# Building the upper list from a complement that GpSimd writes, in the second attention of a two-layer model

## The reference, cut to what matters

```python
draft = jnp.einsum('bhqd,bhkd->bhqk', qr, kr)
causal_future = qi[:, None] < ki[None, :]
draft = draft + jnp.where(causal_future, neg, jnp.asarray(0.0, dtype))
num_remain = max(min(Sq, MIN_REMAIN), Sq - int(Sq * MASK_OUT))     # 128
_, draft_indices = jax.lax.top_k(draft, num_remain)
mask = mask.at[b_idx, h_idx, s_idx, draft_indices].set(0.0)
mask = jnp.where(causal_future[None, None, :, :], neg, mask)
scores = jnp.einsum('bhqd,bhkd->bhqk', qr, kr) / np.sqrt(HD).astype(np.float32) + mask
attn = jax.nn.softmax(scores, axis=-1)
out = jnp.einsum('bhqk,bhkd->bhqd', attn, v)
```

## Time and profile before

| | us |
|---|---|
| median of 3 runs (2258.46 to 2261.43) | 2259.57 |
| the profiled execution | 2258.43 |
| its span | 2256.6 |
| TensorE matmuls busy | 1860.4 (82%) |
| VectorE busy | 1500.8 (67%) |
| ScalarE busy | 1181.4 (52%) |
| GpSimd busy | 802.9 (36%) |

### The profile page before, as it was taken

How to read it: one execution, slowest core, us unless ns; L and a number is a source line. 1 busy time by engine, 2 the same in 40 slices (tenths; PEclk the granted TensorE clock), 3 DMA queues, 4 the chain that set the end, 5 groups by cost and what they waited for, 6 DMA issues and landing times. The chain is left out here.

```text
span 2256.6 us, 27824 instructions
## 1 busy us (share of the span) xinstructions
PE 1860.4 (82%) x8600; PEld 1331.2 (59%) x8600; DVE 1500.8 (67%) x3325; ACT 1181.4 (52%) x2969; POOL 802.9 (36%) x523
## 2 busy tenths in 40 slices
PE   5898999988999769999765777778777777777997
PEld 4777777777777648887652443333444333335885
DVE  3677777777777644555652788888788888723335
ACT  3556656566565432333326677876677676242221
POOL 3445445455453435565321111112311112123442
PEclk9999999999999979999775778879887888887998
DMA  4011111111110112221240000010000000001111
GB/s 159 25 53 60 65 67 43 52 59 71 60 47 21 61 56 102 94 84 56 98 105 17 15 15 15 15 29 11 18 15 15 15 15 15 0 0 52 51 42 51
DMA packets 48722, 104.11 MB, mean 46 GB/s; under 512 B 6672, under 2 KB 30864, under 8 KB 44432
## 3 DMA queue, kind: packets, MB, share of 16 engines
q1 hardware_dynamic: 48624, 102.95, 13.7%
HBM read 95.59 MB, written 7.34 MB: 46 GB/s over the span
## 5 line engine op out<-in xcount | busy, mean ns | idle before, releaser
L225 PE MATMUL PS<-XT,AR 128*128 128x512 f32 x2472 | 620.2, 406 | 25.9 <-POOL AR L833 12.3
L225 PE MATMUL PS<-AR 128*128 128x512 f32 (+2 forms) x2568 | 540.7, 365 | 24.8 <-POOL AR L342 13.2
L225 PEld LDWEIGHTS PS<-XT,AR 128*128 128x128 f32 x2472 | 471.3, 193 | 139.4 <-issue 16.7
L225 PEld LDWEIGHTS PS<-AR 128*128 128x128 f32 x2568 | 441.5, 192 | 117.8 <-POOL AR L342 16.2
L1436 POOL TENSOR_TENSOR AF<-AF 128x512 f32<-128x512 f32 (+3 forms) x64 | 148.4, 2320 | 675.0 <-DVE AF L1668 675.0
L1610 DVE MAX8 BF<-PS 128x8 f32<-128x256 f32 (+2 forms) x384 | 196.7, 555 | 60.7 <-PE PS L1233 59.1
L1376 ACT ACTIVATE AF<-PS 128x512 f32<-128x512 f32 x160 | 92.5, 595 | 268.6 <-PE PS L1244 191.5
L1258 PE MATMUL PS<-AF,BF 128*128 128x512 f32 x320 | 190.3, 699 | 28.8 <-ACT AF L1376 28.6
L586 POOL TENSOR_TENSOR AF<-AF 128x512 f32<-128x512 f32 (+1 forms) x64 | 107.5, 1680 | 169.2 <-DVE AF L717 169.2
L580 POOL TENSOR_TENSOR AF<-AF 128x512 f32<-128x512 f32 x80 | 103.3, 1292 | 169.3 <-ACT AF L372 169.3
L1212 PE MATMUL PS<-AR,XT 48*128 48x128 f32 (+3 forms) x256 | 94.9, 454 | 73.3 <-DVE BF L1538 40.7
(11 more groups left out here) (195 smaller groups left out, 3451.2 us busy)
## 6 DMA issues: line engine op xcount, KB each, us to landing
AF<-in_mean_w SPq DMA_DIRECT2D x48, 448.0 KB, 3.3
AF<-in_ffn_w SPq DMA_DIRECT2D x14, 1536.0 KB, 6.6
AF<-in_attn_w SPq DMA_DIRECT2D x9, 1536.0 KB, 8.1
XT<-rope_scratch SPq DMA_DIRECT2D x180, 64.0 KB, 2.8
AF<-in_attn_w SPq DMA_DIRECT2D x9, 1024.0 KB, 5.0
AF<-in_ffn_w SPq DMA_DIRECT2D x11, 769.0 KB, 4.2
rope_scratch<-BF SPq DMA_DIRECT2D x20, 256.0 KB, 2.3
AF<-in_x SPq DMA_DIRECT2D x8, 256.0 KB, 4.1
```

Of the source, the lines that this page charges most:

```text
L225: last = nc.tensor.matmul(dst, lhs(a, c), rhs(m, c), start=(first and k == 0), stop=(k == 3 * n - 1 and not more))
```

## The change

GpSimd gets a third task, `complement`: it reads each mark as soon as it is written and writes mark minus one, 0 where marked and -1 elsewhere, in bf16 into one of two buffers `rest`. 2^126 times this is the same as what L1226 and L1228 build with two matmuls, so one matmul of `big_b` with `rest` takes their place. Its sixteen instructions for a tile stand in GpSimd's code ahead of the tile's four `norm`; from the third head on each also waits until TensorE has read the buffer two heads before. On TensorE the two matmuls of the under list now come first, then the wait for `rest`, then the one matmul of the over list, then the two score matmuls. The constant `less_big` and ScalarE's conversion of it go.

```diff
-        less_big = SG[:, 1536:2048]
+        rest = [SG[:, 1536:2048], SG[:, 3328:3840]]
...
-            pe.wait_ge(A1["mask_b"], 5)
+            pe.wait_ge(A1["mask_b"], 4)
...
+                pe.wait_ge(A1["above"], 16 * before(x) + h + 1)
+                under = slot(listed(x, h, 0))
+                nc.tensor.matmul(under[:, 0:W], negbig_b, above[:, h % 3, 0:W], start=True, stop=False)
+                nc.tensor.matmul(under[:, W - P:W], ident_b, mask_b, start=False, stop=False)
+                pe.wait_ge(A1["rest"], 16 * before(x) + h + 1)
                 over = slot(listed(x, h, 1))
-                nc.tensor.matmul(over[:, 0:W], ident_b, less_big[:, 0:W], start=True, stop=False)
-                pe.wait_ge(A1["above"], 16 * before(x) + h + 1)
-                nc.tensor.matmul(over[:, 0:W], big_b, mark, start=False, stop=False)
-                under = slot(listed(x, h, 0))
-                nc.tensor.matmul(under[:, 0:W], negbig_b, mark, start=True, stop=False)
-                nc.tensor.matmul(under[:, W - P:W], ident_b, mask_b, start=False, stop=False)
+                nc.tensor.matmul(over[:, 0:W], big_b, rest[h % 2][:, 0:W], start=True, stop=False)
...
-            nc.scalar.activation(less_big, bigs[:, 0:SEQ], ACT.Copy).then_inc(A1["mask_b"], 1)
...
+            def complement(x, h):
+
+                W = tile_of(x)[3]
+                k = 16 * before(x) + h
+                pool.wait_ge(A1["above"], k + 1)
+                if h >= 2:
+                    pool.wait_ge(A1["ring_full"], listed(x, h - 2, 1) + 1)
+                nc.gpsimd.tensor_scalar(rest[h % 2][:, 0:W], above[:, h % 3, 0:W], -1.0, None, ALU.add)\
+                    .then_inc(A1["rest"], 1)
...
             for x in range(NB):
+                if tile_of(x)[1] > 0:
+                    for h in range(16):
+                        complement(x, h)
                 for q in range(4):
                     norm(x, q)
```

More of the change, by code:

```diff
@@ L986, in build_kernel @@
                    "tables", "vproj", "v", "vz", "stored0", "stored1", "kst_first", "kst_rest0", "kst_rest1", "kst0", "kst1", "kst2", "kst3", "qst0", "qst1", "qst2", "mask", "mask_b",
-                   "ring_full", "ring_free", "kneg", "above", "tiny", "nmax", "thr", "acc", "cut", "tau",
+                   "ring_full", "ring_free", "kneg", "above", "rest", "tiny", "nmax", "thr", "acc", "cut", "tau",
                    "flag_ps", "exp", "final", "rinv", "pnorm", "turned", "pt", "pv", "o_hi", "o_lo", "yproj", "yadd")
@@ L1515, in dve_attn1 @@
             dve.wait_ge(A1["mask"], 112)
-            dve.wait_ge(A1["mask_b"], 5)
+            dve.wait_ge(A1["mask_b"], 4)
             for s in range(2):
```

## The result

The change made the kernel slower by about 1%: 2287.64 us (median of four executions, 2284.54 to 2289.62) beside 2260.50 for the kernel before, ratio 1.0110 with a 95% interval from 1.0087 to 1.0132. On another chip, later, it was 2284.82 beside 2266.10, ratio 1.0088 (1.0070 to 1.0106). The direction was forecast, the size was not: I had +10 us (2269.5 us, with a range of 2257 to 2282), and it is 19 to 27 us. Three executions among all the runs lie far outside their kernel's others (2678, 3498 and 6814 us); they are left out of every ratio.

The account below looks back on a forecast made before the run. VectorE's mark and two MAX8 per head were taken to bound the list stage. Terms -5.6 + 3.9 + 9.25 + 2.5 gave +10 us, 2268.4 from the profiled execution; the median's 1.1 us more made it 2269.5 us, range 2257 to 2282.

Parts of the forecast that it names:

- the projections: Waits behind the output projection in six tiles: one matmul less and the earlier under list save 5.6 us together.
- the tile starts: First list of each tile waits for its complement, partly won back in later heads: together +3.9 us, negation tiles apart.
- Price of the complement: GpSimd's new instruction, priced from the key negation: 1.48 us at 512 columns, 1.16 at 384, 0.83 at 256.
- the cheap complement: Rival: GpSimd's complement costs only what the cast does (0.61, 0.48, 0.35 us); about 0, 2260 us; chance 0.16.
- GpSimd as the pace: Rival: complements make lists late in every head; 2290 us at 1.25 times the price, above 2330 at 1.5; chance 0.12.
- The negations: Tiles 7 and 8: first complement queues behind GpSimd's key negation, +4.4 and +4.85 us net, together +9.25 us.
- The win-back of one matmul in each late head: After a tile's late first list, TensorE regains one matmul per late head, about 0.22 us at 512 columns.
- The collisions: VectorE's threshold update behind head 6 stretched by a running complement, in seven tiles: +2.5 us.
- The rival "faster": The earlier ring slot pays at all 58 VectorE waits, some 28 us saved: 2253.5 us; chance 0.08.
- a change of granted clock without a sign: TensorE's clock in the second attention's stretch might change and hide the sum either way; no size or chance given.

Follow-up runs that it names:

- hybrid: The change with the old two over matmuls in heads 0 to 4 of each tile, complements only from head 5: 2274.26 us, ratio 1.0059.
- fillers: Against the change with negations moved: six copies of the under matmul before TensorE's wait for a tile's first complement; 2292.69 us, ratio 1.0136 to the kernel before.

## Why the prediction was wrong

The sum was +10 us from a trace with a stretch of 707.9 us; the change measured +27.1 there. In short: the step that put the projections at -5.6 us failed, and the tile starts were sized too small. By its own steps:

- **Price of the complement: right**, to 0.02 us. The negation was the right row to go by, and the cheap complement is out. (One row of before is dearer an element than the negation, 1250 ns for 448 elements on L591, but only as long as the fixed part is counted in.) **GpSimd as the pace** is out as well: the usual heads are 1.47 us apart at 384 columns.
- **The negations: right in kind, and near in size.** First MAX8 of tiles 7 and 8 5.8 and 5.6 us later, forecast 5.7 and 5.5; with what was to be won back 4.4 and 4.85. Moving the negations gave 5.7 us, the rest of that term is an ordinary late start.
- **The tile starts: right in kind, too small.** All that isn't a projection wait grew by 18.6 us in the list stages, where the starts and negations had 13.2. The hybrid gives 16.9 for them. The win-back of one matmul in each late head is the part that failed: 1.7 us instead of 0.8 in tiles 5 and 11, where TensorE ran part of these heads at 1.2 GHz. (That the wait for the complement brings this about is argued, not shown: it is gone with fillers, but an added wait alone left both tiles at 1.00.) The order costs about 1 us more.
- **The projections: wrong, and the largest miss.** The step that failed is "the six projection tiles give 0.5, 0.6, 1.9, 0.5, 1.1 and 1.0, together -5.6 us". (How 1.1 and 1.0 come about isn't shown there; at 2.4 GHz its own rule gives 0.6 and 0.8.) Waits behind the projections were 2.1, 1.6, 3.6, 2.1, 4.2 and 1.3 us before, and are 4.4, 3.1, 2.5, 4.6, 3.0 and 2.5 now: 15.0 became 20.1, +5.1 instead of -5.6. Part of this is the trace that I started from: counting every wait from the projection to the end of its tile, the three traces of before have 15.3, 20.8 and 18.1 us and the two of the change 20.1 and 20.4, so that against the mean it is +2.2 instead of -5.6. One matmul less alone has 20.2 and 20.4, and seven matmuls ahead of the projections bring it to 11.8 in the change and 11.1 in before. I priced each at the clock that it had in the trace of before, though the earlier trace rows showed a wait of 3.62 us in tile 6 that I had myself put down to the lower clock. What I took for a property of the tile is a draw, and with one matmul less in each head it is always the bad one (0 of 48).
- **The collisions: wrong, 2.5 us too much.** The threshold update in the midst of a complement (GpSimd, then VectorE, tile 6 of after):

```profile
1493.55 1.49 POOL L1457 TENSOR_SCALAR SG<-SG 128x512 bf16<-128x512 bf16 x1 [0.37 <-DVE SG L1613]
...
1494.59 0.16 DVE L1586 SCALAR_TENSOR_TENSOR BF<-BF,SG 128x16 f32<-128x16 f32 x1
```

It takes 0.16 us with two inputs from SBUF, 1.04 us into the complement and 0.45 before its end; nine such updates lie inside a complement, all of 0.16 to 0.18 us. I had carried a rule over from the scaling behind the f32 normalization (2.26 us) to another pair of instructions. The Trainium skill (SBUF — State Buffer, "Who interferes with whom") expects contention of an instruction with two SBUF inputs with a GpSimd instruction that reads SBUF; for this pair the rows show none.
- **Gaps between tiles**: +3.4 us, for which I had nothing. The traces of before differ among themselves by 2.4 us here (340.6 to 343.0), so little of it is sure.

So 10.7 us at the projections, 5.5 at the starts and 3.4 in the gaps, less 2.5 for the collisions, are the 17.1 that were missing. About 3 of these aren't the change's: the trace that I started from was the best of three (mean 710.9). The experiments split the other 24.3 us of the change in another way: 2.8 us from before to one matmul less, 4.7 from there to the hybrid, and 16.9 from the hybrid to the change. So most of what the change costs is the late first lists and the negations, which I had in kind; the projections are where my sum was furthest off, because the gain that was to pay for them never came. **The rival "faster"** is out by the run with the order alone. The prediction does name the cause of its largest miss, in its last lines, as a change of granted clock without a sign. A hint of the sign could be had: work was taken from an engine that the earlier trace rows show at either level in the same stage, and the trace had four projections at 3.0 us and two at 4.5 and 4.9, in tiles of the same shape. I didn't ask why they differ.

What stays open: why the clock holds or falls in one projection tile of before and not in the next, why seven matmuls in the late heads of all tiles go with longer gaps, what the hybrid loses beside one matmul less (4.7 us), and what sets the level behind the last list. That the projections cost the change what they cost is shown by its run with seven matmuls (stretch -9.3 us); that the lower level comes from less work ahead of them, by the counts in the table and by the kernel before with seven, which gains. How the clock is set from that work, no run here shows.

## What to carry to other kernels

Taking work from an engine that isn't the bound is not free if its clock follows its work: look at stages of the same shape in one trace, and where they have two lengths and two granted clocks, price the stage at both levels, and ask which way the change pushes. Before putting a small step onto an engine with an in-order queue, look for what is in front of it at each stage's start; the mean spacing in the middle of a stage doesn't tell. And a sum against one trace inherits that trace's draws: two more traces of the kernel before would have put 3 us of this miss where it belongs.

## What the runs showed of the hardware

- An instruction of GpSimd with one bf16 input and a constant takes 848, 1168 and 1488 ns for 256, 384 and 512 elements a partition, 2.5 ns an element and 0.21 us fixed. It is no cheaper an element than the tensor_scalar from f32 (5363 ns for 2048 elements, on 48 partitions).
- TensorE at five, six and seven matmuls a head had the twelve projection matmuls at 2.4 GHz in 0 of 48, 19 of 36 and 23 of 24 tiles. First lists 0.9 to 2.2 us later by an added wait didn't lower this (4 of 6).
- Repeating a matmul whose result is thrown away made a kernel faster by 0.27% (0.16 to 0.38%).
- A threshold update with two SBUF inputs wasn't stretched inside a bf16 GpSimd instruction (0.16 to 0.18 us in nine tiles), and small VectorE instructions behind the f32 normalization were (2.26 us in tile 7 of before, and as much in after).
